# A two-layer graph attention kernel: both layer norms written as scale times x plus shift on ScalarE, the edge mask as ones times a diagonal, and a new order of stages

## What is computed

```python
# layer 0: one head, masked by adj == 0
q = x @ Wq + bq;  k = x @ Wk + bk
scores = where(adj == 0, -1e18, q @ k.T / 16)
attn = where(adj == 0, 0.0, softmax(scores))
y = layernorm(x + (attn @ x) @ Wc) * gamma + beta
# layer 1: eight heads of 32 channels, adj as a factor
q, k, v = y @ Wq.T + bq, y @ Wk.T + bk, y @ Wv.T + bv
logits = q @ k.T / sqrt(32) + log(clip(adj, 1e-8))
out = softmax(logits) @ v
result = layernorm(y + out @ Wo.T + bo) * gamma + beta
```

## Time and profile before

| | |
|---|---|
| time, median of 3 runs | 1361.48 us (1360.1 to 1369.71) |
| profiled execution, its own time | 1357.96 us |
| its span | 1355.9 us |
| TensorE busy | 1195.1 us (88%), mean granted clock 0.932 |
| VectorE busy | 1011.2 us (75%) |
| GpSimd busy | 763.8 us (56%) |
| ScalarE busy | 523.8 us (39%) |

### The profile page before, as it was taken

The page is one execution under the profiler, slowest core; times in us unless marked ns, Lnnn a source line. Parts: engine busy times, 40 slices in busy tenths (PEclk is TensorE's granted clock), DMA queues, the critical chain, the costliest instruction groups (busy, mean ns, idle before and its releaser), DMA issues.

```text
span 1355.9 us, 21107 instructions
## 1 busy us (share of the span) xinstructions
PE 1195.1 (88%) x6458; PEld 708.8 (52%) x6474; DVE 1011.2 (75%) x1728; ACT 523.8 (39%) x1004; POOL 763.8 (56%) x359
## 2 busy tenths in 40 slices
PE   6889889898998889999989989989899998999963
PEld 4655454554645455564645556454555645465421
DVE  4365867778687787878879786877878787787863
ACT  2223344334343343434434343434334344444330
POOL 0016458384654747476574846548374755848583
PEclk8779999899999899998989999999899999999876
DMA  3041231404123050321305041231504123140300
GB/s 117 0 120 37 60 96 44 128 16 119 52 57 98 16 139 32 95 76 50 105 16 145 25 120 51 58 97 38 133 16 114 56 62 93 45 126 16 93 16 15
DMA packets 69651, 94.66 MB, mean 70 GB/s; under 512 B 14081, under 2 KB 32769, under 8 KB 69634
## 3 DMA queue, kind: packets, MB, share of 16 engines
q1 hardware_dynamic: 69634, 94.44, 25.1%
HBM read 35.40 MB, written 8.39 MB: 32 GB/s over the span
## 4 chain that ended last, share of the span: by engine, by line
PE 35%; POOL 19%; SPq 16%; issue 10%; DVE 9%; DMA 6%; ACT 3%; POOLq 0%; ACTq 0%; DVEq 0%
SPq L407 15%; POOL PR L1101 10%; DMA ADJ<-adj_t 6%; PE misc L559 5%; PE misc L624 4%; PE values L701 4%; PE misc L611 3%; PE scores L680 3%; POOL z L1113 3%; POOL res L1086 3%; POOL res L1084 3%; DVE BIAS L935 3%; PE misc L569 2%; DVE xn L1001 2%; PE values L728 2%
## 5 line engine op out<-in xcount | busy, mean ns | idle before, releaser
L1101 POOL TENSOR_TENSOR PR<-PR,CLIP 128x1024 f32<-128x1024 f32 x224 | 559.5, 2514 | 485.1 <-ACT PR L805 484.9
L805 ACT ACTIVATE PR<-scores 128x512 f32<-128x512 f32 x512 | 278.0, 596 | 279.8 <-PE scores L680 276.0
L962 DVE TENSOR_REDUCE mx<-misc 128x1 f32<-128x512 f32 x512 | 320.2, 679 | 80.7 <-PE misc L659 78.5
L680 PE MATMUL scores<-QS,KS 97*128 97x512 f32 x512 | 201.5, 471 | 17.9 <-ACT PR L805 12.9
L701 PE MATMUL values<-PR,V 128*32 128x512 f32 x1024 | 143.6, 634 | 31.8 <-POOL PR L1101 31.8
L701 PE MATMUL denominators<-PR,ones 128*32 128x512 f32 x1024 | 144.8, 639 | 3.1 <-POOL PR L1101 3.1
L680 PEld LDWEIGHTS scores<-QS,KS 97*128 97x128 f32 x512 | 91.1, 201 | 107.2 <-ACT PR L805 60.1
L659 PE MATMUL misc<-K1H,Q1H 32*128 32x512 f32 x512 | 117.2, 500 | 8.7 <-DVE mx L962 3.4
L637 PE MATMUL misc<-U,P 128*128 128x257 f32 x512 | 123.2, 389 | 0.0
L1009 DVE RECIPROCAL sums_w<-sums_w 128x128 f32<-128x128 f32 x128 | 113.9, 923 | 6.2 <-ACT sums_v L815 6.2
L659 PEld LDWEIGHTS misc<-K1H,Q1H 32*128 32x128 f32 x512 | 49.5, 183 | 112.2 <-DVE mx L962 62.5
(11 more groups left out here) (158 smaller groups left out, 2005.7 us busy)
## 6 DMA issues: line engine op xcount, KB each, us to landing
ADJ<-adj_t SPq DMA_DIRECT2D x16, 1024.0 KB, 6.0
QS<-Q1H SPq DMA_DIRECT2D x256, 64.0 KB, 2.0
KS<-K1H SPq DMA_DIRECT2D x256, 64.0 KB, 2.0
P<-x_t SPq DMA_DIRECT2D x16, 512.0 KB, 3.9
X<-x SPq DMA_DIRECT2D x16, 512.0 KB, 3.7
QS<-Q1L SPq DMA_DIRECT2D x128, 64.0 KB, 2.0
KS<-K1L SPq DMA_DIRECT2D x128, 64.0 KB, 2.0
out<-z SPq DMA_DIRECT2D x16, 512.0 KB, 2.9
```

The costliest lines, as they stand in the source:

```text
L680: pe.matmul(ST[n][:], KS[:, h, P * k:P * (k + 1)], QS[:, h, :], start=True, stop=True).then_inc(scores_filled, 1)
L805: act.activation(PR[quad % WEIGHT_BUFFERS][:, h, :], ST[n][:], ACT.Exp, scale=SCALE1).then_inc(exp_done, 1)
L962: dve.tensor_reduce(mx1[:, g, h, t:t + 1], misc_bank(ph, "max1", g, n)[:], AX.X, ALU.max, negate=True).then_inc(misc_drained["dve"], 1)
L1101: pool.tensor_tensor(w, w, clipped, ALU.mult).then_inc(masked_pool, 1)
```

## The change

Five edits, and a new order of all stages:

1. `norm0` and `norm1`: VectorE now computes only centre = -mean x rstd, one instruction of 128x4 each; ScalarE does the four instructions of 128x256, each as Identity(scale x + bias) with scale and bias read from a column per partition.
2. `bias`: the tensor is now ABSENT, 1.0 where there is no edge, and the instruction also writes a sum along its row (accum_out), which nobody reads.
3. The diagonal that it is multiplied with holds -1e18 (`masked_bf`) instead of 1.
4. `sums_out` copies the values first, then the denominators.
5. `values1(4)` waits for the copy of the values only, and each of the two banks waits for its own copy.

The core of the diff:

```diff
-    ("u", 3), ("max1", 1, 2), ("floor",), ("max1", 1, 3), ("project",), ("shift0",), ("scores1", 2, 0),
+    ("low_output", 1), ("max0", 3), ("u", 3), ("max1", 1, 2), ("floor",), ("scores1", 2, 0), ("max1", 1, 3),
...
-                pe.matmul(bank[:], ident_bf[:], BIAS[:, k, :], start=False, stop=True).then_inc(misc_filled, 1)
+                pe.matmul(bank[:], masked_bf[:], ABSENT[:, k, :], start=False, stop=True).then_inc(misc_filled, 1)
...
-                    elif k == 0:
-                        pe.wait_ge(sums_out, (ph.i * GROUPS + g) * 2)
+                if quad > 0 and k == 0:
+
+                    pe.wait_ge(sums_out, (ph.i * GROUPS + g) * 2 - (1 if bank is PV else 0))
...
+                act.copy(sums_v[:], PV[:]).then_inc(sums_out, 1)
                 act.copy(sums_w[:], DEN[:]).then_inc(sums_out, 1)
-                act.copy(sums_v[:], PV[:]).then_inc(sums_out, 1)
...
+            def norm0(ph):
+                act.wait_ge(centre0_ready, ph.j + 1)
+                if ph.back:
+
+                    act.wait_ge(res_ready, ph.i + 1)
+                for t in range(T):
+                    act.activation(xn[:, t, :], X[:, t, :], ACT.Identity, bias=centre0[:, t:t + 1],
+                                   scale=rstd0[:, t:t + 1]).then_inc(xn_ready, 1)
+
+            def norm1(ph):
+                act.wait_ge(centre1_ready, ph.t + 1)
+                for t in range(T):
+                    act.activation(z[:, t, :], z[:, t, :], ACT.Identity, bias=centre1[:, t:t + 1],
+                                   scale=rstd1[:, t:t + 1]).then_inc(zn_ready, 1)
...
-            dve.tensor_copy(ident_bf[:], ident[:]).then_inc(ident_ready, 1)
+            dve.tensor_scalar(masked_bf[:], ident[:], MASKED, None, ALU.mult).then_inc(ident_ready, 1)
...
-                dve.tensor_scalar(BIAS[:], ADJ[:], 0.0, MASKED, ALU.is_equal, ALU.mult).then_inc(bias_built, 1)
+                dve.tensor_scalar(ABSENT[:], ADJ[:], 0.0, None, ALU.is_equal, ALU.add,
+                                  accum_out=absent[:]).then_inc(bias_built, 1)
...
             def norm0(ph):
                 dve.wait_ge(rstd0_ready, ph.j + 1)
-                if ph.back:
-
-                    dve.wait_ge(res_ready, ph.i + 1)
-                for t in range(T):
-                    dve.tensor_scalar(xn[:, t, :], X[:, t, :], mv0[:, t, 0:1], rstd0[:, t:t + 1],
-                                      ALU.subtract, ALU.mult).then_inc(xn_ready, 1)
+                dve.scalar_tensor_tensor(out=centre0[:], in0=mv0[:, :, 0], scalar=-1.0, in1=rstd0[:],
+                                         op0=ALU.mult, op1=ALU.mult).then_inc(centre0_ready, 1)
```

More of the change, by code:

```diff
@@ L60 @@
 SCHEDULE = [
-    ("split", 0), ("split", 1), ("reciprocal", 1, 0), ("reciprocal", 1, 1), ("max1", 1, 0), ("max1", 1, 1),
[13 rows of a table removed]
-    ("reciprocal", 0, 0), ("scores1", 6, 0), ("transpose", 0), ("transpose", 1), ("scores1", 6, 1),
-    ("reciprocal", 0, 1), ("reciprocal", 0, 2), ("reciprocal", 0, 3), ("values1", 5), ("prepare", 2),
+    ("split", 0), ("split", 1), ("reciprocal", 1, 0), ("max1", 1, 0), ("reciprocal", 1, 1), ("q0", 0),
[13 rows of a table added]
+    ("transpose", 0), ("denominators1", 4), ("reciprocal", 0, 0), ("scores1", 6, 0), ("transpose", 1),
+    ("scores1", 6, 1), ("reciprocal", 0, 1), ("reciprocal", 0, 2), ("reciprocal", 0, 3), ("values1", 5),
     ("q1", 0), ("k1", 0), ("q1", 1), ("scores1", 7, 0), ("denominators1", 5), ("normalise", 0),
[4 rows of a table removed]
[4 rows of a table added]
     ("max1", 0, 14), ("max1", 0, 15), ("sums_out", 1), ("v", 1), ("mrow1", 0),
@@ L221, in two_layer_graph_attention @@
         ident = sb("ident", [P, P])
-        ident_bf = sb("ident_bf", [P, P], BF16)
+        masked_bf = sb("masked_bf", [P, P], BF16)
         ones = sb("ones", [P, P])
@@ L244, in two_layer_graph_attention @@
         ADJ = sb("ADJ", [P, T, N])
-        BIAS = sb("BIAS", [P, T, N], BF16)
+        ABSENT = sb("ABSENT", [P, T, N], BF16)
+        absent = sb("absent", [P, 1])
         Q0H, Q0L = (sb(n, [P, C, N], F32R) for n in ("Q0H", "Q0L"))
@@ L260, in two_layer_graph_attention @@
         rstd0 = sb("rstd0", [P, T])
+        centre0 = sb("centre0", [P, T])
         xn = sb("xn", [P, T, D])
@@ L289, in two_layer_graph_attention @@
         rstd1 = sb("rstd1", [P, T])
+        centre1 = sb("centre1", [P, T])
         WQT, WKT, BQ_WIDE = res[:, 0:C, :], res[:, C:2 * C, :], xn[:, 0:C, 0:P]
@@ L334, in two_layer_graph_attention @@
         rstd0_ready = sem("rstd0_ready")
+        centre0_ready = sem("centre0_ready")
         xn_ready = sem("xn_ready")
@@ L354, in two_layer_graph_attention @@
         rstd1_ready = sem("rstd1_ready")
+        centre1_ready = sem("centre1_ready")
         zn_ready = sem("zn_ready")
@@ L612, in max0 @@
                 for k in range(T):
-                    mm = pe.matmul(bank[:, P * k:P * (k + 1)], BIAS[:, k, q], ident_bf[:],
+                    mm = pe.matmul(bank[:, P * k:P * (k + 1)], ABSENT[:, k, q], masked_bf[:],
                                    start=False, stop=(k == T - 1))
@@ L825, in xn_high @@
                 act.copy(XNH[:, c, :], misc_bank(ph, "transpose", c)[:]).then_inc(hi_written, 1)
+            def norm0(ph):
[10 more added lines that the diff above has]
+                                   scale=rstd1[:, t:t + 1]).then_inc(zn_ready, 1)
             do = {
-                "prepare": prepare, "split": split,
+                "prepare": prepare, "split": split, "norm0": norm0, "norm1": norm1,
                 "q0": lambda ph, c: hi(ph, "q0", c, Q0H, BQ0),
@@ L1041, in norm1 @@
                 dve.wait_ge(rstd1_ready, ph.t + 1)
-                for t in range(T):
-                    dve.tensor_scalar(z[:, t, :], z[:, t, :], mv1[:, t, 0:1], rstd1[:, t:t + 1],
-                                      ALU.subtract, ALU.mult).then_inc(zn_ready, 1)
+                dve.scalar_tensor_tensor(out=centre1[:], in0=mv1[:, :, 0], scalar=-1.0, in1=rstd1[:],
+                                         op0=ALU.mult, op1=ALU.mult).then_inc(centre1_ready, 1)
             do = {
```

## The result

| | before | after |
|---|---|---|
| time, median of 4 runs each | 1365.06 us | 1420.54 us (1413.42 to 1425.94) |
| ratio, with its 95% interval | | 1.0433 [1.0366, 1.0499] |
| profiled execution, its span | 1355.9 us | 1424.1 us |
| mean granted clock | 0.932 | 0.910 |
| mean of 13 steady periods | 79.1 us | 83.3 us |

Slower by 4.3%, where the prediction said 1376 us and a range up to 1396. The sign was right; the size was not: 1.0 us a period was forecast and 4.2 came.

The account below looks back on a forecast made before the run. TensorE, busy 88%, can win only idle and low-clock time. Pieces 10.85 + 49.7 + 18.6 plus half of 1.5 gave 79.9 us a period against 78.9; times 15, plus 2 for filling and draining, led to 1376 us, range 1330 to 1396.

Parts of the forecast that it names:

- ABSENT: VectorE's edge mask with the sum: 2.4 us, no more waiting for GpSimd, so `max0` starts at 10.85 in every period.
- The clock at `max0`: TensorE's idle 1.8 us before `max0` may bring the low clock; half of 1.5 us a period charged.
- norm1 on ScalarE: Four instructions behind layer 0's last exponential take 2.0 us, so GpSimd's `output` starts 1.6 us later.
- the 0.55 for the moved scores: `scores1(1, 1)` now runs ahead of `max0`; its 0.55 us was taken off the end of layer 0's last exponential.
- M: The start of `max0`, from which later steps of a period are timed; `output` was predicted 23.1 us after it.
- GpSimd from `output` to rstd: GpSimd's stretch: 18.85 us, plus 0.5 for VectorE's mask (4, 0) falling between the two residual operations.
- The last context tile's early place gives nothing: Moving that TensorE stage earlier wins 0, since its statistics were not what GpSimd waited for.
- rstd to `q1`: Centre, norm0, exponentials and mask of (5, 1), then values to `q1`: 7.2 us, `q1` 2.5 behind the good period.
- The rest: From `q1` to the next turning of the maxima: same stages, left at 18.6 us.
- Slower still: Rival with full charges, 1.5 us for clock and 1.1 for the mask: 1395 us; no separate chance, slower overall 0.40.
- 0.6 us for slower instructions: Cost each time of moving norm1 from VectorE to ScalarE, by the skill's rule alone: 2.0 us for four against 1.38.

Follow-up runs that it names:

- norm1_alone: The kernel before with only norm1 moved to ScalarE, its centre on VectorE; 1385.7 us, ratio 1.011.
- order_alone: The kernel before with only the new list of stages, norms, mask and copies as before; 1414.8 us, ratio 1.035.
- back_list: The kernel before with the old list as far as the first context tile and the new list behind it; 1372.2 us, ratio 1.011.
- free_context_back: The changed kernel with both norms on VectorE in two sum-writing steps, and the last context tile back behind scores1(4, 1); 1401.9 us, ratio 1.024.
- edits_alone: The changed kernel, all five edits, with the old list of stages; 1399.9 us, ratio 1.024.
- norms_alone: The kernel before with only the two norms moved to ScalarE, old list; 1399.3 us, ratio 1.023.

## Why the prediction was off, step by step

- *ABSENT*: right. 2.29 us and 0.08 for reading out the sum, in all 16 graphs (2.4 taken); `max0` at 10.97 (10.85). That it brings nothing by itself was right too.
- *The clock at `max0`*: half of 1.5 taken. Between 181 and 1100 us of after, 7 of 12 periods have a low stretch of 3.4 us or more from `max0` on, in the one shown above behind 1.86 us of idle time. Right within some tenths.
- *norm1 on ScalarE*: 2.06 for four (2.0), and in norm1_alone `output` is 2.2 us later between periods of one kind (23.7 for 21.5 behind `max0` where the clock stays up, 25.2 for 23.0 where it falls). The 1.6 were these 2.15 less the 0.55 for the moved scores. Right. But `output` started at M + 25.8 in the mean, not 23.1, and this is the first step that failed: I took 0.55 off for the moved scores and left everything else ahead of the context tile at its old length. The 0.55 never came, the front half of the list made the piece 1.2 us longer in the mean, and the low clock behind `max0`, which the sum charges by itself, is the rest: it moves `output` by 1.5 (21.5 to 23.0 in the kernel before). I had read the list only at the three places where an edit stood.
- *GpSimd from `output` to rstd*: 19.35 taken, 19.6 measured. "The last context tile's early place gives nothing" held in the changed kernel, where `output` keeps GpSimd busy until mask (4, 1). Where GpSimd is on time it costs 1.25 to 1.5, as order_alone, back_list and free_context_back show.
- *rstd to `q1`*: 7.2 taken, 8.3 in the mean (9.2 in the rows above). This is the second step that failed. I wrote that TensorE idles there "and that work comes when xn is there", and gave it no price, because I took the chain over ScalarE and GpSimd for the longer one. TensorE's own row of work, at half speed, is longer: 8.34 us without a wait. My 7.2 was right for the old list: in edits_alone, with the same edits, rstd to `q1` is 7.2 in the mean. A stage moved in front of work that used to fill a wait costs that work, and costs it at the low clock.
- *The rest*: 18.6, measured 18.61.
- The sum: 2.7 too little to `output`, 0.25 to rstd, 1.1 to `q1`, 0.1 to `max0`, less the 0.75 for the clock that lies within the first: 3.4 us a period, 83.3 in place of 79.9. Times 15 that is 51 us; the time was 44.5 above the forecast.
- *Slower still* (1395) came nearest, but its two charges were not what made up the rest. The Trainium skill's advice that I had set beside norm1 (ScalarE: Activation LUTs, Rules for kernel authors) pointed the right way: norms_alone is 2.3% slower. But the price that I had put beside it, 0.6 us for slower instructions, is not what was paid: four take 2.06 us on ScalarE against 3.05 for norm1 on VectorE, caught by GpSimd. What cost is the late start of `output` behind the exponentials.

## To carry to other kernels

When a list is reordered, walk TensorE's row of work between two waits, not only the chains over the other engines: whatever no longer fills a wait comes behind it, at the clock that the wait left. Where a VectorE instruction of one input varies in length by whole GpSimd operations, look at it before anything else: it makes distances of 0.4 us decide over 2 to 4, so that any edit upstream may look good or bad by chance. The form that also writes a sum ended it here and made the kernel 1.5% faster, even with two instructions in place of one. And a caught instruction costs only what its reader waits.
